# Two attentions of one fused block on one NeuronCore: an image's normalisation one burst later on ScalarE, the transposes of its result two bursts later on TensorE

## What is computed

```python
x = _L0_conv_ref(x, L0_conv_Wb, L0_conv_Wc, L0_conv_Wd, L0_conv_gamma)
x = x + _L1_conv_ref(_gn(x), L1_conv_W_qkv, ..., L1_conv_W_proj, L1_conv_b_proj)   # 8 heads of 16, softmax over 256 keys
t = _to_tokens(x)
t = t + _L2_attn_ref(_ln_t(t))                                                     # needs layer norm of every token
t = t + _L2_ffn_ref(_ln_t(t), ...)
t = t + _L3_attn_ref(_ln_t(t), rope_cos, rope_sin, W_q, W_k, W_v, W_o, ...)        # 8 heads, causal window of 32 keys
t = t + _L3_ffn_ref(_ln_t(t), ...)
```

## Time and profile before

| what | value |
|---|---|
| median of three runs | 785.45 us |
| profiled execution, its own time | 785.37 us |
| its span in the trace | 783.4 us |
| TensorE busy | 623.1 us (80%) |
| VectorE busy | 460.1 us (59%) |
| ScalarE busy | 338.7 us (43%) |
| GpSimd busy | 252.5 us (32%) |

### The profile page before, as it was taken

The page is one execution under the profiler, slowest core; times in us unless marked ns, Lnnn a source line. Parts: engine busy times, 40 slices in busy tenths (PEclk is TensorE's granted clock), DMA queues, the critical chain, the costliest instruction groups (busy, mean ns, idle before and its releaser), DMA issues. The chain is left out here.

```text
span 783.4 us, 10991 instructions
## 1 busy us (share of the span) xinstructions
PE 623.1 (80%) x3298; PEld 342.2 (44%) x3298; DVE 460.1 (59%) x1096; ACT 338.7 (43%) x569; POOL 252.5 (32%) x468
## 2 busy tenths in 40 slices
PE   3783989888266589999999999974569999566997
PEld 2662544555155554444334344322444566352332
DVE  1587455674158457768868968954943566224433
ACT  1441224665133166665665675643531455312222
POOL 5111000233300037765666675654400133310000
PEclk9996996999578589999999999996858999757999
DMA  1055000000010000000000000000000000000000
GB/s 40 27 174 117 1 1 1 2 2 1 7 34 14 1 0 0 1 0 1 1 0 0 0 0 0 0 0 0 2 0 1 2 2 2 1 2 0 13 13 27
DMA packets 11440, 9.59 MB, mean 12 GB/s; under 512 B 4218, under 2 KB 9348, under 8 KB 11396
## 3 DMA queue, kind: packets, MB, share of 16 engines
q1 hardware_dynamic: 11396, 9.04, 4.0%
HBM read 6.94 MB, written 1.05 MB: 10 GB/s over the span
## 5 line engine op out<-in xcount | busy, mean ns | idle before, releaser
L1256 POOL TENSOR_TENSOR h_s<-g_s 128x512 f32<-128x512 f32 x128 | 162.6, 1273 | 97.5 <-ACT g_s L1240 93.4
L1215 DVE TENSOR_TENSOR z_s<-bank,PB 128x1024 f32<-128x1024 f32 x128 | 155.8, 1224 | 57.8 <-PE bank L1182 50.2
L1240 ACT ACTIVATE g_s<-z_s,b 128x1024 f32<-128x1024 f32 x128 | 147.2, 1150 | 85.5 <-DVE z_s L1215 83.7
L1189 PE MATMUL bank<-h_s,W 128*128 128x512 f32 x256 | 132.3, 600 | 6.5 <-ACT y_s L1235 4.1
L1182 PE MATMUL bank<-XN_C,W 128*128 (+1 forms) x256 | 131.0, 596 | 1.0 <-PEq L1112 1.0
L888 DVE TENSOR_REDUCE shiftpad<-bank 128x2 f32<-128x512 f32 (+1 forms) x128 | 72.3, 588 | 72.5 <-PE bank L723 43.2
L871 ACT ACTIVATE ET_all<-bank 128x512 f32<-128x512 f32 (+1 forms) x128 | 58.9, 512 | 91.5 <-PE bank L740 48.5
L1189 PEld LDWEIGHTS bank<-h_s,W 128*128 128x128 f32 x256 | 47.4, 191 | 73.5 <-issue 49.3
L1182 PEld LDWEIGHTS bank<-XN_C,W 128*128 128x128 f32 x256 | 48.5, 192 | 59.4 <-issue 57.8
L937 POOL TENSOR_SCALAR var<-mv 128x2 f32<-128x2 f32 x16 | 3.5, 220 | 189.5 <-DVE mv L926 189.5
L735 PE MATMUL bank<-Qp,Kp 17*128 17x256 f32 x256 | 39.0, 420 | 4.9 <-DVE Qp L899 4.8
(11 more groups left out here) (251 smaller groups left out, 1074.5 us busy)
## 6 DMA issues: line engine op xcount, KB each, us to landing
W<-in_L_ffn_W_dram SPq DMA_DIRECT2D x1, 2048.0 KB, 8.6
xs<-in_x_dram SPq DMA_DIRECT2D x8, 128.0 KB, 2.1
xs<-XN_C SPq DMA_DIRECT2D x8, 128.0 KB, 2.0
out_dram<-y_s SPq DMA_DIRECT2D x4, 256.0 KB, 2.1
Wgate<-in_L_ffn_W_gate_dram SPq DMA_DIRECT2D x1, 256.0 KB, 4.1
Wup<-in_L_ffn_W_up_dram SPq DMA_DIRECT2D x1, 256.0 KB, 4.8
Wdown<-in_L_ffn_W_down_dram SPq DMA_DIRECT2D x1, 256.0 KB, 4.4
wraw<-in_L_conv_W_qkv_dram SPq DMA_DIRECT2D x1, 192.0 KB
```

The costliest lines, as they stand in the source:

```text
L1189: nc.tensor.matmul(bank[7][:, :], W2[:, f % FT, :], h_s[:, f % RING, :], start=(f % FT == 0), stop=(f % FT == FT - 1)).then_inc(s_D.sem, 1)
L1215: nc.vector.tensor_tensor(z_s[:, s % RING, :].rearrange("p (w n) -> p w n", w=2), bank[s % 4][:, None, :].broadcast_to([P, 2, W]), PB[:, b ...
L1240: nc.scalar.activation(g_s[:, s % RING_G, :], z_s[:, s % RING, :], ACT.Gelu, bias=b1[:, s:s + 1]).then_inc(s_g.sem, 1)
L1256: nc.gpsimd.tensor_tensor(h_s[:, s % RING, :], g_s[:, s % RING_G, 0:W], g_s[:, s % RING_G, W:2 * W], ALU.add).then_inc(s_h.sem, 1)
```

## The change

Two lags go up: `AT_XN` from 14 to 15 and `AT_XT` from 15 to 17. By that the normalisation L863 of image n stands in burst 4n+15, and its transposes L801 with the copy L858 in burst 4n+17. The order in which bank 7 goes round changes with it (shifts, then the transposes L801, then those of `o_n`, shifts, projection), so three waits are replaced: L801 now waits until the shifts of the burst before have been added and until the projection of image n+1 has been taken out (`s_r`); the transposes of `o_n` of image n wait for the copy of image n-2 (`s_done` n-1); the projection no longer waits for `s_done`.

```diff
-        AT_OT, AT_ON, AT_Y, AT_XN, AT_XT = 8, 9, 11, 14, 15
+        AT_OT, AT_ON, AT_Y, AT_XN, AT_XT = 8, 9, 11, 15, 17
...
                         if (n := image_at(s, AT_XT)) is not None:
                             pe.wait_ge(s_xn, n + 1)
-                            pe.wait_ge(s_sh, min(2 * n + 7, HALVES))
-                            pe.wait_ge(s_oTs, min(n + 2, IMAGES))
+                            pe.wait_ge(s_sh, min(2 * n + 8, HALVES))
+                            pe.wait_ge(s_r, min(n + 2, IMAGES))
...
                             if n >= 1:
                                 pe.wait_ge(s_r, n)
+                            if n >= 2:
+                                pe.wait_ge(s_done, n - 1)
...
                         if (n := image_at(s, AT_Y)) is not None:
                             pe.wait_ge(s_oTs, n + 1)
                             pe.wait_ge(s_sh, min(2 * n + 5, HALVES))
-                            if n >= 1:
-                                pe.wait_ge(s_done, n)
```

## The result

The changed kernel takes 769.25 us, the median of six runs (762.24 to 781.57); the kernel before, run beside it, 787.15 us (783.54 to 811.03). The ratio is 0.9732, with a 95% interval of 0.9678 to 0.9786. (Executions that stand out as disturbed are left out of every ratio here, not out of the medians.) Put on the 785.45 us of the prediction that is 764.4 us, 760.2 to 768.6: about 21 us faster. I had forecast 771.0 us, 14.4 us faster, and 766.5 to 776.5.

A forecast was written before the change was run, and what follows sets the result against it. Bound in the middle by TensorE together with the loop through the query add, at the ends by one chain through all engines. 0.93 + 0.75 + 5.48 + 7.28 = 14.4 us off 785.45 gives 771.0 us, range 766.5 to 776.5.

The forecast's parts named there:

- The middle: Images 0 to 4 of each attention: shorter TensorE waits give 0.93 us in layer 1 and 0.75 us in layer 3.
- The 0.39 us: Middle images: part of TensorE's idle time that comes back per image; the rest becomes a wait for VectorE's query add.
- ScalarE's gap: Middle: the normalisation fits ahead of burst 4m+3's exponentials with 0.35 us to spare, so it costs nothing.
- The end of layer 1: Last images of layer 1: earlier values and an earlier projection of image 7 give 0.77 + 4.71 = 5.48 us.
- Second step: Ends: image 7's projection comes sooner, GpSimd's chains 6 and 7 start 4.45 us apart; 4.71 us in layer 1, 4.70 in layer 3.
- First step: Ends: burst 34's exponentials no longer wait behind image 5's normalisation; 0.77 us in layer 1, 1.58 + 1.00 us in layer 3.
- The end of layer 3: Last images of layer 3: closer chains, earlier values and a clock that stays up give 4.70 + 1.58 + 1.00 = 7.28 us.
- What I can't price from a row: Behind both attentions: clock changes may fall on other instructions; 3 us to either side, from three runs 5.8 us apart.
- A: Middle: transposed scores need not wait for the query add, each image gives its whole idle time; 765.1 us, chance 0.07.
- B: Ends: image 7's projection is late for another reason, chains stay 9.2 us apart; 783.7 us, chance 0.08.
- C: Middle: normalisation misses its gap before burst 4m+3's exponentials by 0.53 us, ten times; 776.3 us, chance 0.04.
- D: Middle: granted clock falls to 1.2 GHz, costing 3.6 us an image; 807 us with all ten middle images, chance 0.03.

The follow-up runs named there:

- middle_only: New lags for images 0 to 4 of both attentions, old ones for images 5 to 7; 784.95 us, ratio to the kernel before 0.9962.
- last_on_vector: Changed kernel with each attention's last image's rstd and shift made by VectorE instead of GpSimd; 764.99 us, ratio to the kernel before 0.9729.
- after: First run and profile of the changed kernel, against the kernel before; 769.25 us, ratio 0.9732.
- again: The changed kernel run and profiled once more, no edit, against the kernel before; 773.93 us, ratio 0.9767.
- end_only: New lags for images 5 to 7 of both attentions, old ones for images 0 to 4; 771.94 us, ratio to the kernel before 0.9817.
- end_driven: Changed kernel with nine extra matmuls, results never read, in TensorE's idle time at each attention's end; 765.71 us, ratio to the kernel before 0.9723.
- before_again: Second profile of the kernel before, no edit; the profiled execution took 781.2 us.
- again_2: The changed kernel run and profiled a third time, no edit, against the kernel before; 770.09 us, ratio 0.9719.
- add_first: Changed kernel with VectorE's query add moved ahead of the row maxima of its burst's first unit, everywhere; 772.09 us, ratio to the kernel before 0.9823.
- add_first_alone: Changed kernel with the query add ahead of the row maxima in bursts 4m+2 only; 774.98 us, too scattered for a ratio.
- vector_both: Changed kernel with the query add first in its burst and the last image's rstd on VectorE; 768.21 us, ratio to the kernel before 0.9745.

## Why the prediction was right and wrong

**The two ways of being bound:** right for the ends, misread for the middle. The idle time before the transposes is 16.8 us, not "about 14". Of that, 14.0 us lie in images 6 and 7, as forecast. The other 2.8 us lie in the middle, where the transposes wait for the query add in their new place.

**The middle:** nearly the right number, from a wrong wait. Forecast 0.93 + 0.75 us, measured 1.6 + 0.7. The wait of 0.81 us against "some 0.8" and the image of 10.17 us against 10.24 came as forecast. But the step "The wait has been there all the time, hidden behind the other" is wrong: there was only one wait, for the query add, with the wrong engine's name on it (0.10 us from add to transposes, 0.62 from normalisation). The 0.39 us were not idle time given back. They were the transposes' own 0.34 us, which stood between the add and the scores, and 0.05 us because the scores follow the add by 0.05 us where the transposes followed it by 0.10. That this sum equals the forecast's is luck, as one start time served for both readings. Over a whole image of layer 1 the idle time went from 0.86 + 0.37 + 0.17 to 0.81 + 0.42 us, so 0.17 us came back, all of it the wait for the scaled output that the moved transposes now cover; the other 0.12 us lie in shorter blocks of scores. In layer 3 an image gained 0.09 us, not 0.15; the first one's 0.38 us filled the sum up. middle_only gives 1.8 us, not 7.6.

**ScalarE's gap:** right; 0.35 us to spare were forecast, 0.48 us of idle time are there. The Trainium skill ("PSUM — Partial Sum Buffer", Engine vs sequencer instructions) calls ScalarE's queue strictly first in, first out. The trace agrees where it costs something, in last_on_vector: image 7's normalisation was ready at 215.6 and ran at 216.12, behind a copy that waited.

**The end of layer 1:** the mechanism right, the sum 1.3 to 1.5 us too large (4.2 and 4.0 us in after and again). Second step 4.68 us (forecast 4.71). First step: forecast 0.77, in the changed kernel -0.47, in end_only 0.74, in end_driven 0.63. I had looked for a fall of the clock only in layer 3; one came here. The 1.17 us of idle time ahead of it don't explain it alone, as the last section shows.

**The end of layer 3:** right. 25.3 - 18.3 = 7.0 us against 7.28; the clock stayed up until the last values and projection were done (0.47 and 0.71 us), as hoped. The first step gave 2.29 us of 2.58, the second 4.67 of 4.70.

**The sum:** 14.4 us forecast, 13.5 in the changed stretches and 0.7 behind them, 14.2 in all. The sum of the path came out. What failed is the step "What I can't price from a row": everything outside the path was put at nothing in the sum, with "I take 3 us to either side for it", sized from three runs that lay 5.8 us apart. Measured, it is 4 to 8 us, all to one side: the ratios of the three comparisons give 21, 18 and 22 us, and the path 14.2. Nineteen runs of the changed kernel span 22 us and 39 of the kernel before 43; the table shows in which stretches. So the range was too narrow for what single executions do, but scatter alone is a weak account of a surplus that has the same sign three times.

**What stays open** is where the 4 to 8 us beyond the path come from. The path alone is a ratio of 0.982, and the first and third interval (up to 0.9786 and 0.9781) exclude it. I resampled the pooled times: 18 us between the medians of all of them, 12 to 23 in 19 of 20 draws, which takes in 14.2; but 19.5 us, 15 to 24, between the medians of those that the ratios use (27 and 11), which does not. One part can be narrowed down. "Between" is 405.9 to 406.0 us in three of the four profiles whose layer 1 ends late (the three of the kernel before and middle_only; before_again has 402.8), and 398.1 to 404.3 us in all ten whose layer 1 ends sooner. The instructions there are the same. In the profiles of the kernel before, the whole 3 us arise at the start of layer 3, with no difference up to there. That may be some 2 us from the clock meeting layer 3's start otherwise when layer 1 ends sooner; but before_again shows the same without the change, and the ten differ by 6 us among themselves. For the rest, no stretch that holds a moved instruction shows it, and no run here says whether it is the change's doing.

**The rivals.** A (all waits come back) is refuted by rows of the profile and by middle_only: the scores do wait for the add, and so did the transposes. B (the ends get no shorter) by 4.48 us. C (ScalarE in the way) by the gap. D (the clock falls in the middle because of the change) did not occur in the images of after and again. In again_2 the clock was down for a whole image, which costs more than I had priced: 16.25 us from chain 0 to chain 1, against 10.12, where I had put 3.6 us an image. That fall began ahead of every moved instruction; whether the change has a part in how long it lasted is not shown, since all three profiles with such an image are of changed kernels.

## What to carry to other kernels

Before pricing a wait that an edit takes away, check that the named releaser ended just before the wait did: here it had ended 0.62 us earlier, and the instruction had a second wait, which ended 0.10 us before it started. Then read what the next instruction waits for. The gain was at the drain of the pipeline, where one projection had stood behind an older image's transposes. Cut the profiles of several executions of the same kernel at common marks; stretches that repeat to a few tenths of a microsecond can be compared from single profiles, while the whole time needs many runs. And size the range of a forecast from the scatter of many runs, not of three.

## What the runs showed of the hardware that I had not expected

- TensorE's clock fell to 1.2 GHz early in layer 1 although TensorE had been busy 10.59 of the 12 us before (again_2, 104 to 116 us), and stayed down through 128 to 152 us with TensorE busy over 11 of every 12 us. In the three stretches from 116 to 152 us before_again stood at 1.00, 0.86 and 1.00, almost wholly at 2.4 GHz. The Trainium skill ("TensorE: Matmul & The Clock Gate", What's actually happening) has activity lift the slow clock; these rows don't agree with that, and the measurement decides. What else holds the clock down here was not tried.
- The same wait of 1.17 us before layer 1's last values was followed by 1.2 GHz in after, again, again_2 and last_on_vector, and by 2.4 GHz in end_only, add_first, add_first_alone and vector_both. A wait of 0.53 us was followed by 1.2 GHz in middle_only, and one of 0.52 or 0.53 us by 2.4 GHz in all three profiles of the kernel before. So the length of the wait does not decide it. With one matmul in the wait whose result nobody reads, the clock stayed up in end_driven, whose order is otherwise that of the four that fell (one profile).
- Nine such matmuls an attention shortened two stretches by 1.4 and 2.1 us.
